# Attention scores in float32r row tiles of 32, with the maxima taken off by a product of their own

## The chip, the cores and the metric

One core of a Trainium2 chip runs the whole kernel. The metric is the device time of one execution in microseconds (us), lower is better. A core has a matrix engine (PE, TensorE), VectorE (DVE), ScalarE (ACT), GpSimd (POOL) and SyncE (SP, which here only issues DMAs). They run side by side and meet at semaphores.

## What is computed

A transformer block over x of shape (4, 512, 128): layer norm, attention with 16 heads of 8 dimensions, a second layer norm and residual, then a gated feed-forward part with layer norm and residual. All is float32. The part that the change touches is the score product and its softmax:

```python
q = (x @ Wq + bq).reshape(b, t, H, hd).transpose(0, 2, 1, 3)
k = ((x @ Wk + bk) @ Wl + bl).reshape(b, t, H, lhd).transpose(0, 2, 1, 3)
v = ((x @ Wv + bv) @ Wl + bl).reshape(b, t, H, lhd).transpose(0, 2, 1, 3)
attn = jax.nn.softmax(jnp.einsum('bhqd,bhkd->bhqk', q, k) * scale, axis=-1)
out = jnp.einsum('bhqk,bhkd->bhqd', attn, v)
```

Here b = 4, H = 16, hd = 8, t = 512. The biases of q and k are large, so the scores need more than bfloat16 accuracy and the row maxima have to be taken off before the exponential.

## The kernel before

Everything is written out by hand: one instruction list per engine, with semaphores between them.

**Groups and blocks.** The 16 heads go in NG = 4 groups of GH = 4. A batch (one of 4) is BLK = 16 blocks: block n belongs to group n // 4 and to key tile t = n % 4 (128 keys). In one block PE does, for each of the 4 heads, one score product for the exponentials (L1262: keys on partitions, 512 queries as columns, into `psB`, which has two banks) and one for the maxima (L1243: queries on partitions, 512 keys as columns, into `psA`, two pairs of banks, of a group that lies LEAD = 6 blocks ahead). Then it multiplies the exponentials of the block before by v (`times_v`, L1274: four heads side by side in column tiles of 32, float32). DVE reduces each pair of `psA` banks to row maxima (L933), two reductions a block. ACT takes each `psB` bank through the exponential (L784), four a block, into `pT`.

**How the scores are made exact enough.** q and k are each split in three bfloat16 parts (`PARTS` = 3). `QS[g]` and `KS[g]` hold in partitions 0 to 71 the nine products of parts by 8 dimensions, zeros up to 95 (KMAX = 96), and in partitions 96 to 98 of `QS` the three bfloat16 parts of the row maxima, against -1 in `KS`. So one bfloat16 product of 96 partitions gives the scores for the maxima, and one of 99 partitions gives the scores less their maxima.

**How the parts get there.** ACT copies q and k out of PSUM twice (L703, L704), POOL (DVE for batch 0) makes the rests (L520, L524, L889 to L898), ACT the second parts (L715); SP writes the parts to DRAM scratch (`q_scr`, `k_scr`, L382) and reads them back, repeated over partitions (L401, L407), 4 DMAs a group. `take_parts` (L696) of batch b waits until batch b-2 has been written (L702).

**Order before the first exponentials.** All four batches' q, k and v are made first, between the first 6 blocks of maxima (the lead, L1310 to L1321). SP's list is: the writes of batch 0, the loads of its four groups, the writes of batch 1 (L440), `put_maxima(0, 0)` (L441), the writes of batches 2 and 3. The first exponential score product waits for `put_maxima(0, 0)`, and that for ACT's `take_first_maxima`, which stands in ACT's list behind `take_q(3)` (L752).

**The maxima of a group.** After its 8 reductions POOL splits them in three parts (`split_maxima`), PE transposes them (`job_m`, L1205), ACT copies (`take_maxima`, L734), SP puts them in place with one DMA (`put_maxima`, L414); the first score product of that group waits for it (L1252).

**Jobs.** Output projection, layer norms and feed-forward of the batch before are placed between the score products, by the table PE_AT (block, place); place 0 is ahead of `for_maxima(1, 0)`, place 1 ahead of `for_exponentials(2)`, place 2 ahead of `for_exponentials(3)`, place 3 ahead of `times_v`, place 4 behind it.

Score bank 0 of `psB` serves heads 0 and 2 and bank 1 heads 1 and 3, so PE's `for_exponentials(2)` waits for the exponential of head 0, and `for_exponentials(3)` for that of head 1 (L1261). In the last 6 blocks of the last batch there are no maxima left, and heads 2 and 3 use `psA`.

Of the kernel before, what the change touches and what calls it, by code (L numbers as in the profile page):

```python
# [23 lines left out]
def sandwich_kernel(nc, x, Wq, bq, Wk, bk, Wv, bv, Wl, bl, Wo, bo, W_r, W_k, W_v, mu_r, mu_k, out):  # L24
    fp32 = mybir.dt.float32
    bf16 = mybir.dt.bfloat16
    u32 = mybir.dt.uint32
# [3 lines left out]
    ds = bass.ds  # L31
# [11 lines left out]
    ROWS = PARTS * PARTS * D  # L43
    KMAX = 96
    KEXP = KMAX + PARTS
# [3 lines left out]
    MINUS_ONES = 0xBF80BF80  # L49

    ctx = ExitStack()
    with ctx:
# [8 lines left out]

        q_scr = nc.dram_tensor("q_scr", [NB, PARTS, D, H, T], bf16, kind="Internal").ap()
        k_scr = nc.dram_tensor("k_scr", [NB, PARTS, D, H, T], bf16, kind="Internal").ap()
# [32 lines left out]
        qf = sb("qf", [P, T])  # L97
        qr = sb("qr", [P, T])
        qp = sb("qp", [P, 2, PARTS, T], bf16)
        kf = sb("kf", [P, T])  # L100
        kr = sb("kr", [P, T])
        kp = sb("kp", [P, 2, PARTS, T], bf16)
# [3 lines left out]
        QS = [sb(f"QS{g}", [P, GH, T], bf16) for g in range(NG)]  # L106
        KS = [sb(f"KS{g}", [P, GH, T], bf16) for g in range(NG)]
# [68 lines left out]
        s_padp = sem("s_padp")  # L176
        s_padv = sem("s_padv")
# [18 lines left out]
        q_r1 = sem("q_r1")  # L196
        q_p1 = sem("q_p1")
        q_p2 = sem("q_p2")
        k_rdy = sem("k_rdy")
        k_tak = sem("k_tak")  # L200
        k_r1 = sem("k_r1")
        k_p1 = sem("k_p1")
        k_p2 = sem("k_p2")
# [3 lines left out]
        q_wr = [sem(f"q_wr{b}") for b in range(NB)]  # L207
        k_wr = [sem(f"k_wr{b}") for b in range(NB)]
        ld = [sem(f"ld{g}") for g in range(NG)]
        LW = PARTS + 1  # L210
# [140 lines left out]

        def later(n):

            return not isinstance(n, int) or n > 0
# [13 lines left out]
        def _(sp):  # L368
# [16 lines left out]
            def write_q(b, i):  # L385
                write_part(b, i, q_scr, qp, (q_tak, q_p1, q_p2)[i], q_wr)

            def write_k(b, i):
                write_part(b, i, k_scr, kp, (k_tak, k_p1, k_p2)[i], k_wr)

            def write_parts(b):
                for i in range(PARTS):
                    write_q(b, i)
                    write_k(b, i)

            def load_q(b, g):
                q_src = q_scr[ds(b, 1), :, :, GH * g:GH * (g + 1), :]
                for i in range(PARTS):
                    r = PARTS * D * i  # L400
                    sp.dma_start(QS[g][r:r + PARTS * D, :, :].rearrange("p h n -> p (h n)"),  # L401
                                 q_src[:, i:i + 1, :, :, :].rearrange("a i d h n -> a (i d) (h n)")
                                 .broadcast_to([PARTS, D, GH * T])).then_inc(ld[g], 16)

            def load_k(b, g):
                k_src = k_scr[ds(b, 1), :, :, GH * g:GH * (g + 1), :]
                sp.dma_start(KS[g][0:ROWS, :, :].rearrange("p h n -> p (h n)"),  # L407
                             k_src.rearrange("a i d h n -> a (i d) (h n)")
                             .broadcast_to([PARTS, PARTS * D, GH * T])).then_inc(ld[g], 16)
# [1056 lines left out]
```

## Time and profile before

| | |
|---|---|
| median of 3 timed runs | 294.33 us (292.95 to 294.61) |
| span of the profiled execution | 292.1 us |
| PE busy | 257.6 us (88%) |
| DVE busy | 218.2 us (75%) |
| ACT busy | 180.4 us (62%) |
| POOL busy | 108.1 us (37%) |
| DMA, mean | 54 GB/s |

The span is from the first to the last instruction of one profiled execution; the page gives no other time for that execution, and the median of the timed runs lies 2.2 us above the span.
### The profile page before, as it was taken

How to read it: one execution, taken by the hardware profiler on the slowest of the kernel's cores; microseconds unless marked ns; L12 is line 12 of the kernel's file. 1: busy time of each engine (PE TensorE's matmuls, PEld its weight loads, DVE VectorE, ACT ScalarE, POOL GpSimd, SP SyncE). 2: the span in 40 equal slices, each digit the busy share in tenths (PEclk: the TensorE clock that was granted, in tenths of full speed). 3: DMA queues.
4: the chain of work that ended last, by engine and by line, in shares of the span. 5: the costliest groups of instructions: out<-in, count | busy, mean ns of one | idle time of the engine just before them, and what ended most of it. 6: DMA issues, size and time to landing. Idle time of an engine off the chain costs nothing.

```text
span 292.1 us, 4845 instructions
## 1 busy us (share of the span) xinstructions
PE 257.6 (88%) x1379; PEld 100.2 (34%) x1379; DVE 218.2 (75%) x384; ACT 180.4 (62%) x351; POOL 108.1 (37%) x236
## 2 busy tenths in 40 slices
PE   7764883099999999999999999999999999898980
PEld 2441541022323232432433334233333433333560
DVE  2695494065888787989889889988998988763545
ACT  2334350566787867687776776777677678695041
POOL 4897370321001011066321344552117155324522
PEclk9686699558999999999999999999999999999798
DMA  4331133160111111110101121010102000000101
GB/s 108 108 109 77 77 125 123 52 198 2 61 39 66 42 46 56 33 77 19 68 27 57 33 88 49 33 66 20 68 12 103 17 1 2 4 1 0 36 2 36
DMA packets 13045, 15.64 MB, mean 54 GB/s; under 512 B 2529, under 2 KB 10722, under 8 KB 13026
## 3 DMA queue, kind: packets, MB, share of 16 engines
q1 hardware_dynamic: 12450, 15.15, 15.5%
q10 hardware_dynamic: 576, 0.26, 0.3%
q8 instruction: 9, 0.15, 0.2%
q14 instruction: 10, 0.08, 0.1%
HBM read 11.01 MB, written 4.19 MB: 52 GB/s over the span
## 4 chain that ended last, share of the span: by engine, by line
PE 72%; DMA 9%; DVE 8%; SPq 4%; ACT 3%; issue 3%; POOL 1%; POOLq 0%; DVEq 0%; ACTq 0%
PE psO L1274 20%; PE psB L1262 20%; PE psA L1243 17%; DMA q_scr<-qp 4%; DVE mx L933 4%; PE psM L1167 3%; PE psM L1173 3%; SPq L382 3%; DMA KS<-k_scr 3%; PE psA L1154 2%; PE psB L1396 1%; DVE er L996 1%; DMA x_all<-in_L_attn_x_dram 1%; PE psO L1186 1%; SPq L401 1%
## 5 line engine op out<-in xcount | busy, mean ns | idle before, releaser
L933 DVE TENSOR_REDUCE mx<-psA 128x2 f32<-128x1024 f32 x128 | 150.8, 1216 | 45.2 <-PE psA L1243 44.8
L784 ACT ACTIVATE pT<-psB 128x512 f32<-128x512 f32 x244 | 133.1, 597 | 41.2 <-PE psB L1262 40.4
L1262 PE MATMUL psB<-QS,KS 99*128 99x512 bf16 x244 | 94.7, 393 | 12.3 <-DMA QS<-mmT 11.9
L1243 PE MATMUL psA<-KS,QS 96*128 96x512 bf16 x256 | 90.7, 391 | 5.7 <-DMA KS<-k_scr 4.4
L1274 PE MATMUL psO<-pT,Vg 128*32 128x512 f32 x512 | 69.1, 611 | 0.4
L1262 PEld LDWEIGHTS psB<-QS,KS 99*128 99x128 bf16 x244 | 23.6, 98 | 92.0 <-ACT pT L784 57.3
L1243 PEld LDWEIGHTS psA<-KS,QS 96*128 96x128 bf16 x256 | 25.2, 100 | 28.7 <-DVE mx L933 6.2
L493 POOL TENSOR_TENSOR mm<-mx,one 128x16 bf16<-128x16 f32 x16 | 3.5, 217 | 43.2 <-DVE mx L933 43.2
L1274 PEld LDWEIGHTS psO<-pT,Vg 128*32 128x32 f32 x512 | 10.2, 108 | 21.8 <-issue 16.9
L532 POOL TENSOR_TENSOR Vg<-v_st,one 128x128 f32<-128x128 f32 x16 | 6.3, 399 | 28.0 <-PE psO L1274 28.0
L703 ACT ACTIVATE qf<-psO,vec 128x512 f32<-128x512 f32 x4 | 2.7, 687 | 18.0 <-DMA q_scr<-qp 13.4
L1154 PE MATMUL psA<-warm 128*128 128x512 bf16 x36 | 11.4, 482 | 1.2 <-DVE warm L905 1.2
L996 DVE RECIPROCAL er<-rr 128x128 f32<-128x128 f32 x12 | 10.7, 924 | 2.3 <-POOL rr L639 2.3
L760 ACT COPY o_sb<-psO 128x512 f32<-128x512 f32 x15 | 8.8, 590 | 4.4 <-PE psO L1274 4.4
L884 DVE TENSOR_SCALAR xh<-x_all,mv_x,rs_x 128x128 f32<-128x128 f32 x16 | 8.0, 653 | 1.9 <-POOL rs_x L500 1.8
L1173 PE MATMUL psM<-ident,o_sb 128*128 128x128 f32 x60 | 9.0, 272 | 0.0
L694 ACT COPY xhT<-psB 128x512 f32<-128x512 f32 x4 | 2.3, 586 | 10.6 <-PE psB L1179 10.6
L520 POOL TENSOR_TENSOR qr<-qf,qp 128x512 f32<-128x512 f32 x3 | 3.5, 1155 | 14.1 <-ACT qp L704 14.1
L1173 PEld LDWEIGHTS psM<-ident,o_sb 128*128 128x128 f32 x60 | 7.5, 141 | 2.9
L506 POOL TENSOR_TENSOR ve_y<-mv_y,eps 128x4 f32<-128x4 f32 x3 | 0.6, 202 | 20.9 <-DVE mv_y L875 20.9
L506 POOL TENSOR_TENSOR ve_f<-mv_f,eps 128x4 f32<-128x4 f32 x3 | 0.6, 201 | 20.5 <-DVE mv_f L875 20.5
L734 ACT COPY mmT<-psM 48x128 bf16<-48x128 bf16 x15 | 3.8, 254 | 4.9 <-PE psM L1205 4.9
(179 smaller groups left out, 293.8 us busy)
## 6 DMA issues: line engine op xcount, KB each, us to landing
QS<-q_scr SPq DMA_DIRECT2D x48, 96.0 KB
KS<-k_scr SPq DMA_DIRECT2D x16, 288.0 KB
q_scr<-qp SPq DMA_DIRECT2D x12, 128.0 KB, 2.3
k_scr<-kp SPq DMA_DIRECT2D x12, 128.0 KB, 2.3
x_all<-in_L_attn_x_dram SPq DMA_DIRECT2D x4, 256.0 KB, 3.4
out_dram<-out_sb SPq DMA_DIRECT2D x3, 256.0 KB, 4.0
QS<-mmT SPq DMA_DIRECT2D x16, 12.0 KB
out_dram<-out_sb SPq DMA_DIRECT2D x2, 128.0 KB, 1.8
```

Source lines behind the costliest of these rows:

```text
L382: sp.dma_start(scr[b, i, :, :, :].rearrange("d h n -> h d n"), parts[:, b % 2, i, :]).then_inc(written[b], 16)
L760: nc.scalar.copy(o_sb[:, :], psO[:, :]).then_inc(o_tak, 1)
L784: nc.scalar.activation(pT[:, n % 2, i, :], score_bank(n, i, last), ACT.Exp, scale=SCALE).then_inc(e_rdy, 1)
L884: last = nc.vector.tensor_scalar(xh[:, b, t, :], x_all[:, b, E * t:E * (t + 1)], mv_x[:, b, t, 0:1], rs_x[:, b, t:t + 1], ALU.subtract, AL ...
L933: nc.vector.tensor_reduce(out=mx[:, g % 2, c:c + 2], in_=psA[:, u, :, :], axis=AX.X, op=ALU.max).then_inc(a_max, 1)
L996: nc.vector.reciprocal(er[:, E * t:E * (t + 1)], rr[:, E * t:E * (t + 1)])\
L1154: nc.tensor.matmul(psA[:, 1, 0, :], warm[:, 0:P], warm[:, :], start=True, stop=True)
L1167: last = nc.tensor.matmul(psM[:, E * t:E * (t + 1)], lhs[:, P * t:P * (t + 1)], rhs, start=True, stop=True)
L1173: last = nc.tensor.transpose(psM[:, P * t:P * (t + 1)], src(t), ident[:, :])
L1243: score = nc.tensor.matmul(psA[:, u, j, :], QS[g][0:KMAX, h, P * t:P * (t + 1)], KS[g][0:KMAX, h, :], start=True, stop=True)
L1262: nc.tensor.matmul(score_bank(n, i, last), KS[g][0:KEXP, i, P * t:P * (t + 1)], QS[g][0:KEXP, i, :], start=True, stop=True).then_inc(b_rdy, 1)
L1274: last = nc.tensor.matmul(psO[QUAD * i:QUAD * (i + 1), :], Vg[:, g, t, i, :], pT[:, n % 2, i, :], start=(t == 0), stop=(t == NT - 1))
```

## The change

q and k are each split in two halves of 12 bits (`HALVES` = 2) by a bit mask: DVE masks the upper half (`top_half`), and POOL (DVE for batch 0) subtracts it for the lower. ACT copies q and k out of PSUM once. The halves stay in SBUF for all batches (`q_hl`, `k_hl`). There is no DRAM scratch: SP copies rows from SBUF to SBUF, eight DMAs a group (four for q, four for k; 32 partitions of 2 KB each), so that the 4 products of halves by 8 dimensions of one head fill 32 partitions, and the four heads of a group the 128. Each score product is one float32r matmul on the 32 partitions of its head.

The maxima are no longer rows of the score product. `MS[g]` holds their three bfloat16 parts at partitions 32i to 32i+2, and a second product of 3 partitions (`less_maxima`), with a tile of -1, adds them into the same bank. They are put there by three DMAs instead of one. The maxima are made in another order (heads 2 and 3, then heads 0 and 1, of one query tile, where it was four query tiles of one head), and `for_maxima(1, 1)` stands ahead of place 1, where it stood behind `for_exponentials(2)`.

```diff
-            def write_part(b, i, scr, parts, made, written):
-                sp.wait_ge(made, 2 * b + 2 if i == 0 else b + 1)
-                sp.dma_start(scr[b, i, :, :, :].rearrange("d h n -> h d n"),
-                             parts[:, b % 2, i, :]).then_inc(written[b], 16)
+            def load_rows(b, g, dst, src, j, half):
+                sp.dma_start(dst[g][j:P:SPREAD, :].bitcast(fp32),
+                             src[QUAD * g:QUAD * (g + 1), half, ds(b * T, T)]).then_inc(ld[g], 16)
+            def load_q(b, g):
+                for j in range(SPREAD):
+                    load_rows(b, g, QS, q_hl, j, j // HALVES)
+            def load_k(b, g):
+                for j in range(SPREAD):
+                    load_rows(b, g, KS, k_hl, j, j % HALVES)
+            def put_maxima(n, g):
+                sp.wait_ge(m_tak, n + 1)
                 for i in range(PARTS):
-                sp.dma_start(QS[g][KMAX:KEXP, :, :].rearrange("p h n -> p (h n)"),
-                             mmT[:, :]).then_inc(m_in, 16)
+                    sp.dma_start(MS[g][i:P:QUAD, :],
+                                 mmT[MC * i:MC * (i + 1), :]).then_inc(m_in, 16)
...
-            write_parts(1)
             put_maxima(0, 0)
-            for b in range(2, NB):
-                write_parts(b)
...
+                for full, parts, hi, lo in ((qf, q_hl, q_hi, q_lo), (kf, k_hl, k_hi, k_lo)):
+                    pool.wait_ge(hi, b + 1)
+                    at = slice(T * b, T * (b + 1))
+                    nc.gpsimd.tensor_tensor(parts[:, 1, at], full[:, b % 2, :], parts[:, 0, at],
+                                            ALU.subtract).then_inc(lo, 1)
...
-                if b >= 1:
-                    act.wait_ge(r1, b)
                 if b >= 2:
-                    act.wait_ge(written[b - 2], 16 * PARTS)
-                nc.scalar.activation(full[:, :], ps[:, :], ACT.Identity, bias=bias).then_inc(taken, 1)
-                nc.scalar.activation(parts[:, b % 2, 0, :], ps[:, :], ACT.Identity,
+                    act.wait_ge(lo, b - 1)
+                nc.scalar.activation(full[:, b % 2, :], ps[:, :], ACT.Identity,
                                      bias=bias).then_inc(taken, 1)
...
+            def top_half(b, full, parts, taken, hi):
+                dve.wait_ge(taken, b + 1)
+                nc.vector.tensor_scalar(parts[:, 0, T * b:T * (b + 1)].bitcast(u32),
+                                        full[:, b % 2, :].bitcast(u32), TOP_BITS, None,
+                                        ALU.bitwise_and).then_inc(hi, 1)
...
+            SPLITS = {0: (top_q, 1), 1: (top_k, 1), 2: (top_q, 2), 3: (top_k, 2), 4: (top_q, 3),
+                      5: (top_k, 3)}
             for a in range(LEAD):
                 for u in range(2):
                     maxima(a // GH, a, a // GH, a % GH, u, False)
+                split, b = SPLITS[a]
+                split(b)
...
-                score = nc.tensor.matmul(psA[:, u, j, :], QS[g][0:KMAX, h, P * t:P * (t + 1)],
-                                         KS[g][0:KMAX, h, :], start=True, stop=True)
+                rows = rows_of(PAIRS[u] + j)
+                score = nc.tensor.matmul(psA[:, u, j, :], QS[g][rows, P * t:P * (t + 1)],
+                                         KS[g][rows, :], start=True, stop=True)
...
-                nc.tensor.matmul(score_bank(n, i, last), KS[g][0:KEXP, i, P * t:P * (t + 1)],
-                                 QS[g][0:KEXP, i, :], start=True, stop=True).then_inc(b_rdy, 1)
+                nc.tensor.matmul(score_bank(n, i, last), KS[g][rows_of(i), P * t:P * (t + 1)],
+                                 QS[g][rows_of(i), :], start=True, stop=False)
+
+            def less_maxima(n, i, last):
+                rows = slice(QUAD * i, QUAD * i + PARTS)
+                nc.tensor.matmul(score_bank(n, i, last), neg[rows, :], MS[n // NT][rows, :],
+                                 start=False, stop=True).then_inc(b_rdy, 1)
...
                     for_exponentials(0)
                     for_maxima(0, 0)
+                    less_maxima(n, 0, last)
                     for_exponentials(1)
                     for_maxima(0, 1)
+                    less_maxima(n, 1, last)
                     jobs(n, 0)
                     for_maxima(1, 0)
+                    for_maxima(1, 1)
                     jobs(n, 1)
                     for_exponentials(2)
-                    for_maxima(1, 1)
+                    less_maxima(n, 2, last)
                     jobs(n, 2)
                     for_exponentials(3)
+                    less_maxima(n, 3, last)
```

The tiles that only the old form needed go too: the padding of `QS` and `KS` with zeros and -1 (POOL L541, DVE L902), ACT's second copies (L704, L715).

## Rows read from the trace of the kernel before

**Rows 1.** The page: busy share of the engines, granted clock in 40 slices.
```profile
PE 257.6 (88%) x1379; PEld 100.2 (34%) x1379; DVE 218.2 (75%) x384; ACT 180.4 (62%) x351; POOL 108.1 (37%) x236
PE   7764883099999999999999999999999999898980
PEclk9686699558999999999999999999999999999798
```

**Rows 2.** Lines by form: shapes, count | busy us, mean ns | idle before, releaser.
```profile
L933 DVE TENSOR_REDUCE mx<-psA 128x2 f32<-128x1024 f32 x128 | 150.8, 1216 | 45.2 <-PE psA L1243 44.8 <-issue 0.2
L784 ACT ACTIVATE pT<-psB 128x512 f32<-128x512 f32 x244 | 133.1, 597 | 41.2 <-PE psB L1262 40.4
L1262 PE MATMUL psB<-QS,KS 99*128 99x512 bf16 x244 | 94.7, 393 | 12.3 <-DMA QS<-mmT 11.9 <-ACT pT L784 0.2
L1243 PE MATMUL psA<-KS,QS 96*128 96x512 bf16 x256 | 90.7, 391 | 5.7 <-DMA KS<-k_scr 4.4 <-DVE mx L933 1.1
...
L520 POOL TENSOR_TENSOR kr<-kf,kp 128x512 f32<-128x512 f32 x3 | 3.5, 1155 | 1.0 <-ACT kp L704 0.9
```

**Rows 3.** Timeline of one block without jobs: start us, us, engine, line, operation.
```profile
82.31 0.39 PE L1262 MATMUL psB<-QS,KS 99*128 99x512 bf16 x1
...
82.54 0.38 PE L1243 MATMUL psA<-KS,QS 96*128 96x512 bf16 x1
82.54 0.10 PEld L1262 LDWEIGHTS psB<-QS,KS 99*128 99x128 bf16 x1
82.74 2.17 ACT L784 ACTIVATE pT<-psB 128x512 f32<-128x512 f32 x4 [0.58 <-PE psB L1262]
...
83.41 0.38 PE L1262 MATMUL psB<-QS,KS 99*128 99x512 bf16 x1
...
83.88 0.39 PE L1262 MATMUL psB<-QS,KS 99*128 99x512 bf16 x1
...
84.20 1.06 PE L1274 MATMUL psO<-pT,Vg 128*32 128x512 f32 x8
...
85.19 0.39 PE L1262 MATMUL psB<-QS,KS 99*128 99x512 bf16 x1
```

**Rows 4.** Timeline of PE: a job, first score products of batches 1, 2, a float32 job.
```profile
106.98 0.60 PE L1173 MATMUL psM<-ident,o_sb 128*128 128x128 f32 x4
...
109.38 0.39 PE L1262 MATMUL psB<-QS,KS 99*128 99x512 bf16 x1
...
163.50 0.39 PE L1262 MATMUL psB<-QS,KS 99*128 99x512 bf16 x1
...
255.08 1.11 PE L1225 MATMUL psM<-xk,w_T 128*128 128x512 f32 x2
```

**Rows 5.** The chain that ended last, before the first exponentials: start us, us, what.
```profile
22.10 7.90 DMA KS<-k_scr
...
43.89 10.30 DMA q_scr<-qp
...
55.73 2.27 DMA QS<-mmT
```

**Rows 6.** Timeline of the start: kf copied, rest, x normalised, DMA issues, first product.
```profile
14.74 0.69 ACT L703 ACTIVATE kf<-psM,b_kl 128x512 f32<-128x512 f32 x1 [1.29 <-PE psM L1192]
...
16.07 0.68 DVE L892 TENSOR_TENSOR kr<-kf,kp 128x512 f32<-128x512 f32 x1
...
16.63 1.24 SPq L382 DMA_DIRECT2D q_scr<-qp  x2
...
23.33 3.27 DVE L884 TENSOR_SCALAR xh<-x_all,mv_x,rs_x 128x128 f32<-128x128 f32 x8 [0.29 <-POOL rs_x L500]
...
58.12 0.58 PE L1262 MATMUL psB<-QS,KS 99*128 99x512 bf16 x1 [11.91 <-DMA QS<-mmT]
```

**Rows 7.** One stretch by engine: us, busy (count) of each, granted clock, DMA share.
```profile
60.00:70.00 10.00, 10.00 (x36) 2.42 (x34) 6.36 (x6) 5.92 (x11) 1.19 (x5) 0.60 0.39 114
```

**Rows 8.** The tile `mmT`: issues of its DMA, ns minimum/median/maximum.
```profile
L414 SPq DMA_DIRECT2D QS<-mmT x16: 698/747/797, 55.7 to 252.6; - x16
```

More of the change, by code:

```diff
@@ L26, in sandwich_kernel @@
     bf16 = mybir.dt.bfloat16
+    f32r = mybir.dt.float32r
     u32 = mybir.dt.uint32
@@ L42, in sandwich_kernel @@
     PARTS = 3
[L43 to L45 removed]
+    HALVES = 2
+    SPREAD = HALVES * HALVES
     QUAD = 32
@@ L96, in sandwich_kernel @@
         xhT = sb("xhT", [P, 2, T])
[L97 to L102, printed above, removed]
+        qf = sb("qf", [P, 2, T])
+        kf = sb("kf", [P, 2, T])
+        q_hl = sb("q_hl", [P, HALVES, NB * T])
+        k_hl = sb("k_hl", [P, HALVES, NB * T])
         v_st = sb("v_st", [P, NB, NT * H * D])
-        QS = [sb(f"QS{g}", [P, GH, T], bf16) for g in range(NG)]
-        KS = [sb(f"KS{g}", [P, GH, T], bf16) for g in range(NG)]
+        QS = [sb(f"QS{g}", [P, T], f32r) for g in range(NG)]
+        KS = [sb(f"KS{g}", [P, T], f32r) for g in range(NG)]
+        MS = [sb(f"MS{g}", [P, T], bf16) for g in range(NG)]
+        neg = sb("neg", [P, P], bf16)
         Vg = sb("Vg", [P, NG, NT, GH, QUAD])
@@ L423, in _ @@
                 load_x(b)
-            write_q(0, 0)
-            write_k(0, 0)
-            write_q(0, 1)
-            write_q(0, 2)
-            write_k(0, 1)
-            write_k(0, 2)
-            sp.wait_ge(q_wr[0], 16 * PARTS)
-            for g in range(NG):
-                sp.wait_ge(s_padp, (1, 4, 7, 10)[g])
-                if g == 0:
-                    sp.wait_ge(s_padv, 2)
+            for dst, src, hi, lo in ((QS, q_hl, q_hi, q_lo), (KS, k_hl, k_hi, k_lo)):
+                for half, made in enumerate((hi, lo)):
+                    sp.wait_ge(made, 1)
+                    for j in range(SPREAD):
+                        if (j // HALVES if dst is QS else j % HALVES) == half:
+                            load_rows(0, 0, dst, src, j, half)
+            for g in range(1, NG):
                 load_q(0, g)
-                if g == 0:
-                    sp.wait_ge(k_wr[0], 16 * PARTS)
                 load_k(0, g)
-            write_parts(1)
             put_maxima(0, 0)
-            for b in range(2, NB):
-                write_parts(b)
-            for b in range(1, NB):
-                sp.wait_ge(q_wr[b], 16 * PARTS)
-                sp.wait_ge(k_wr[b], 16 * PARTS)
+            sp.wait_ge(q_lo, NB)
+            sp.wait_ge(k_lo, NB)
+            sp.wait_ge(q_hi, NB)
+            sp.wait_ge(k_hi, NB)
             def batch(b, first, last):
@@ L925, in _, with maxima @@
             x_normalise(3)
-            def maxima(group, a, g, h, u, free):
+            def maxima(group, a, g, t, u, free):
                 dve.wait_ge(a_rdy, a * 2 + (u + 1))
-                if h == 0 and u == 0 and free:
+                if t == 0 and u == 0 and free:
                     dve.wait_ge(m_p2, group - 1)
-                c = NT * h + 2 * u
-                nc.vector.tensor_reduce(out=mx[:, g % 2, c:c + 2], in_=psA[:, u, :, :],
+                h = PAIRS[u]
+                into = mx[:, g % 2, :].rearrange("p (h t) -> p h t", t=NT)[:, h:h + 2, t]
+                nc.vector.tensor_reduce(out=into, in_=psA[:, u, :, :],
                                         axis=AX.X, op=ALU.max).then_inc(a_max, 1)
@@ L1234, in job_f, with rows_of, scores_for_maxima @@
                 product_by_tile(kact, w_T[:, T_WVF, :], f_rdy)
-            def scores_for_maxima(e, a, g, h, u, j, free=False):
-                if u == 0 and j == 0 and h == 0:
+            def rows_of(h):
+                return slice(QUAD * h, QUAD * (h + 1))
+            def scores_for_maxima(e, a, g, t, u, j, free=False):
+                if u == 0 and j == 0 and t == 0:
                     pe.wait_ge(ld[g], (e + 1) * (16 * LW))
```

132 lines of the change are left out of this document (38 added, 94 removed).

## The prediction

> **What bounds the kernel now.** I read the page first, for the engine shares and the granted clock. PE is busy in nearly every slice from 60 us on, DVE 75% and ACT 62% over the whole, and the clock sinks only in the first quarter [rows 1]. So there are two parts to price: the start, up to the first score product for exponentials at 58.12 us [rows 6], and the steady part of 64 blocks behind it.
>
> In the steady part I went from the forms [rows 2] to one block without jobs [rows 3]. It runs from 82.31 to 85.19: 2.88 us. Two sums give the same 2.88. By PE alone: products start 0.22 apart (82.31 to 83.41 is five of them), eight take 1.76, the last one keeps `times_v` waiting 0.32 instead of 0.22, and `times_v` takes 0.99 (84.20 to 85.19). That is 1.76 + 0.03 of waiting + 0.10 + 0.99. By the exponentials: the first score product starts at 82.31, ACT begins at 82.74 (0.43 later), two exponentials take half of the 2.17, 1.09, the product of head 3 starts 0.05 behind the second of them (83.88), then 0.32 and 0.99. That is 0.43 + 1.09 + 0.05 + 0.32 + 0.99 = 2.88. Work taken from PE alone thus gives nothing: this second chain stays. DVE needs 2.4 us a block for two reductions (2 x 1.216 [rows 2]) and is not the bound in such a block. A middle batch takes 163.50 - 109.38 = 54.1 us [rows 4]; 16 x 2.88 = 46.1, so its jobs cost 8.0.
>
> At the start two stretches of waiting stand out in the chain: the load of `KS` (7.90 us) and a write of `q_scr` (10.30 us), which holds ACT, and behind it the first maxima [rows 5]. The first product waited 11.91 us [rows 6].
>
> **The change part by part: a steady block.** It adds four products (`less_maxima`), twelve in place of eight. Each must follow its own score product, in the same rows and the same bank, so it can't lie beside it: 0.22 each. Two of them are on the chain of the exponentials whatever else overlaps: that of head 0 ahead of the first exponential, that of head 3 ahead of `times_v`. The chain becomes 0.22 + 0.43 + 1.09 + 0.05 + 0.22 + 0.32 + 0.99 = 3.32 us, 0.44 more.
>
> Whether PE itself fits in that depends on the row tiles. The trace of before has no row tile and no float32r. The nearest row for tiles is `times_v`: eight instructions of 512 columns, four column tiles of two float32 instructions each, in 0.99 us [rows 3]. One float32 product of 512 columns on the full array, two instructions, has 1.11 us [rows 4], so four one after another would need near 4. Tiles do lie side by side here. If row tiles do the same, the twelve products take six slots of 0.22 (first score with first maxima product, then `less_maxima` with the next pair, and so on): 1.3 us, which hides in the 3.32. If they don't, PE is the bound: 12 x 0.22 + 0.10 + 0.99 = 3.73. The price of a block is thus between 3.32 and 3.73; below 3.32 it can't go unless `less_maxima` costs nothing. I take 3.32, since the nearest row shows tiles side by side. For a float32r product the bound from below is the bfloat16 spacing of 0.22, from above the float32 product, 1.0; one of its two instructions, about 0.45, lies between. I take 0.22: it is a single instruction of four-byte numbers whose mantissas are cut to 12 bits, which stands nearer to the bfloat16 row than to the pair that full float32 needs.
>
> On tiles the Trainium skill (TensorE: Matmul & The Clock Gate, Part 3) says that matmuls in different row groups run side by side, and gives 3.07x for four of K = 32 and N = 512; by this the block is at 3.32, and the trace shows the same for column tiles only. The same section says that a weight load overlaps a running matmul only if its row group differs. By that each `less_maxima` would also show its weight load, 0.10 by the row of a load here, and the block would be 3.52. The trace speaks against it: at 82.54 the load for a product of 99 rows runs beside a product of 96 of the same rows [rows 3], and the starts stay 0.22 apart.
>
> **Jobs.** The new block leaves PE idle from 0.86 (its first eight products issued, if side by side) to about 1.24, when the first exponential has freed its bank. Jobs at places 0, 1 and 2 (four transposes take 0.44: 106.98 to the next product [rows 4]) fill this gap in part. But a job uses the full array, so each needs two changes of tiling, which I put at 0.12 each by the 0.10 and 0.12 around `times_v`. Place by place: the four small ones at places 0 to 2 cost 0.2 each or less instead of 0.44, `f` 0.4 instead of 0.9, those at places 3 and 4 their own time plus 0.12. The sum is 5.5 us a batch instead of 8.0.
>
> **Maxima put in place by three DMAs.** One issue takes SP 0.75 us [rows 8], so the last starts 1.5 us later, and it lands 2.3 us after its start [rows 5]. ACT's copy of `m2` and `m4` ends about when block 7 or 15 begins, and the group is needed one block later: 1.5 + 2.3 = 3.8 against 3.32, a wait of 0.5 each. `m1` in batch 0 is 0.5 later still; in later batches the jobs of block 3 hide it. Some 4 us over the kernel. SP is not late elsewhere: 8 loads of a group at 0.6 to 0.75 are 5.5 us and stand ahead of a `put_maxima` that comes three blocks later.
>
> **Steady sum.** Batch 0: 16 x 0.44 = 7.0, waits 1.9, its few jobs -0.5: +8.4. Batches 1 and 2: 16 x 3.32 = 53.1, jobs 5.5, waits 0.9 = 59.5 against 54.1: +5.4 each. Batch 3: ten such blocks +3.4, and six without maxima, where five slots replace four, +1.3. Together +24.
>
> **The start.** Until the copy of kf at 14.74 nothing changes. Then: no second copy by ACT; DVE masks and subtracts (0.45, put between a copy and a subtraction, and 0.68 [rows 6]), done by 16.8. SP issues the first eight copies at 0.62 to 0.75 from 14.7 on, to about 19.9, landed 2 us later. The first scores can start near 22 instead of 30.0. DVE isn't free then: it still has the normalising of x, which ended at 26.6 [rows 6] and moves up by the third parts and casts that it loses and the memsets of POOL beside it, to 24.3. Eight reductions are 9.7, four masks 1.8: the first group's maxima stand at 35.8, the k half of batch 2 is masked last. POOL has its subtraction (1.155 [rows 2]) ahead of the split of the maxima in its list; split 1.2, transpose, copy 0.7, issues 1.5, landing 2.3: the first exponential score product near 43.8 instead of 58.1. The writes of `q_scr` and their 10.3 us are gone. That is -14.3. What is late next: the reductions of DVE, then SP, whose 32 loads end between 35 and 39. The granted clock was 0.60 from 60 to 70 us, mostly the lower of its two levels (1.2 of 1.2 and 2.4 GHz), after PE had stood for 11.9 us [rows 6, 7]; after a wait of 2 us it may not fall. Batch 0 took 109.38 - 58.12 = 51.3 where full clock would give some 49.5: -1.7. The start gives -16; I hold -10 to -20 for possible.
>
> **Sum.** 292.1 + 24 - 16 = 300, with the 2.2 us between span and median 302.3; I say 302.5. Its own range is 295 to 312.
>
> **Rivals.**
> 1. *Row tiles don't overlap here.* A block takes 3.73, and the jobs keep their 8.0 and gain 2.6 of tiling changes: batch 0 +14.5, batches 1 and 2 +16 each, batch 3 +15, the start -16: +46, 340 us. For it: no row shows row tiles, and scores and `less_maxima` mix two types. Against it: `times_v`. 25%.
> 2. *float32r takes as long as one instruction of the float32 pair, 0.43.* With overlap, the chain gets 0.22 more for head 0 and for head 3: 3.76 a block, about 335. Without, PE has 8 x 0.43 + 4 x 0.22 + 1.09 = 5.4 a block, over 430. 12% and 3%.
> 3. *The start pays for all.* The place is the stretch before 58.12: the writes and loads through DRAM vanish. It decides if the first exponential score product comes before 34, or if it comes at 41 and the steady cost is only 16. The chain of reductions alone (24.3 + 9.7) makes the first impossible without DVE freed earlier; the second needs jobs hidden better than I have it. It gives 288 to 291. 8%, and 5% for no difference.
> 4. *The clock falls in the steady part*, since quarter tiles use less of the array: every slot 0.43. Over 400 us. 2%.
>
> **How the numbers follow.** Forecast (side by side, 0.22, slower) 45%; the rivals 25, 15, 8 + 5 and 2%. The range of 8 in 10 leaves out the worst cases (5%) and most of rival 3: 293 to 342. A measurement of this kernel can tell about 0.5% from no change. Faster by over 0.5%: 8%; within: 5%; slower: 87%.
>
> **What would show it.** Side by side: starts of a score product and of the maxima product behind it well under 0.22 apart; else rival 1. The distance from a score product of head 0 to its exponential: 0.65, where it is 0.43. Block period 3.3 (forecast), 3.7 (rival 1 or 2). First exponential score product at 44. Waits for the DMA of `mmT` of 0.5 about twice a batch. DVE less busy by share than 75%. The prediction is wrong if the product of head 3 no longer waits for the exponential of head 1, or if the period of a block is under 3.2.

## The result, and the profile after

The changed kernel takes 423.13 us (median of 4 executions, 422.91 to 425.22) where the kernel before takes 294.47 (4 executions, 292.95 to 295.38): a ratio of 1.4375, 95% interval 1.4313 to 1.4437. The profiled execution has a span of 421.1 us against 292.1, so 129.0 us are to be found. The forecast was 302.5 with a range up to 342. The sign was right and the size was not: the time is that of rival 4, which had 2%.

From the page of the changed kernel: busy share of the engines, and PE's share and the granted clock in 40 slices. It answers to [rows 1].

```profile
span 421.1 us, 5372 instructions
PE 392.9 (93%) x1633; PEld 148.6 (35%) x1635; DVE 217.5 (52%) x386; ACT 175.2 (42%) x337; POOL 92.4 (22%) x221
PE   7888999999999999999999999999999999999893
PEclk9895555555555555556655555556655565557989
```

DVE and ACT do the same number of microseconds of work as before (217.5 and 175.2, before 218.2 and 180.4). PE's went from 257.6 to 392.9, and the last line says why: the granted clock stands near 0.5, the lower of its two levels (1.2 and 2.4 GHz), in nearly all of the span from the fourth slice to the 36th. Before it was at full level in nearly all slices from the tenth on [rows 1]. The mean over the span is 0.592, before 0.932.

The costliest groups of the same page (busy us, mean ns of one, idle before and its releaser), which answer to [rows 2]:

```profile
L869 DVE TENSOR_REDUCE mx<-psA 128x2 f32<-128x1024 f32 x128 | 152.1, 1220 | 162.6 <-PE psA L1186 162.4
L716 ACT ACTIVATE pT<-psB 128x512 f32<-128x512 f32 x244 | 133.0, 596 | 167.8 <-PE psB L1213 162.3
L1207 PE MATMUL psB<-QS,KS 32*128 32x512 f32 x244 | 115.4, 757 | 12.0 <-ACT pT L716 12.0
...
L1213 PE MATMUL psB<-MS,neg 3*128 3x512 bf16 x244 | 97.0, 616 | 0.0
```

One reduction and one exponential are as long as before (1220 and 596 ns; 1216 and 597 in [rows 2]), but both engines now wait about 162 us for PE, before about 45 and 40. In these lines `f32` is also what the float32r products show, one instruction each (numbers of four bytes, here halves of 12 bits); L1207 and L1186 are the score and the maxima products, L1213 is `less_maxima`, L1225 `times_v`.

Two stretches side by side, in the columns of [rows 7] (us, busy and count of PE, PEld, DVE, ACT, POOL, granted clock, DMA share, GB/s). First a middle batch of the kernel before, then the same batch of the changed one:

```profile
121.31:175.24 53.93, 53.69 (x311) 19.51 (x311) 48.43 (x77) 39.28 (x77) 21.23 (x52) 1.00 0.14 51
```
```profile
147.77:242.75 94.98, 91.35 (x375) 32.92 (x374) 49.49 (x76) 40.15 (x77) 21.22 (x52) 0.54 0.10 26
```

By such marks (the first score product for exponentials, then in three batches the start of the job that multiplies `w_in` by `oT`) the 129.0 us lie as follows: start 58.12 to 39.42, -18.7; first product to first mark 63.2 to 108.35, +45.2; two batches 107.7 to 189.7, +82.0; the rest 63.1 to 83.6, +20.5.

A block without jobs, timeline of the changed kernel (start us, us, engine, line, operation), which answers to [rows 3]:

```profile
54.46 0.79 PE L1207 MATMUL psB<-QS,KS 32*128 32x512 f32 x1
54.46 0.79 PE L1186 MATMUL psA<-KS,QS 32*128 32x512 f32 x1
54.47 0.79 PE L1207 MATMUL psB<-QS,KS 32*128 32x512 f32 x1
54.47 0.79 PE L1186 MATMUL psA<-KS,QS 32*128 32x512 f32 x1
55.06 0.65 PE L1213 MATMUL psB<-MS,neg 3*128 3x512 bf16 x2
...
55.74 1.09 ACT L716 ACTIVATE pT<-psB 128x512 f32<-128x512 f32 x2 [0.92 <-PE psB L1213]
...
58.05 1.94 PE L1225 MATMUL psO<-pT,Vg 128*32 128x512 f32 x8
59.91 0.79 PE L1207 MATMUL psB<-QS,KS 32*128 32x512 f32 x1
```

Four products in four row tiles start within 0.01 us of each other, so row tiles do lie side by side; rival 1 is out. But the block takes 59.91 - 54.46 = 5.45 us in place of 2.88, `times_v` 1.86 in place of 0.99, and the first exponential starts 1.28 after its score product in place of 0.43.

Where does the clock fall? In the lead, and from there to about 380 us it comes back only for moments of a few us, of which one is shown (columns as above):

```profile
30.00:32.00 2.00, 0.62 (x4) 0.33 (x4) 2.00 (x4) 0.58 (x2) 2.00 (x3) 1.00 0.40 108
32.00:34.00 2.00, 2.00 (x6) 0.74 (x6) 2.00 (x3) 0.52 (x1) 0.80 (x2) 0.87 0.39 105
34.00:36.00 2.00, 1.26 (x7) 0.17 (x5) 0.33 (x1) 0.16 (x1) 1.37 (x5) 0.50 0.38 100
...
192.00:194.00 2.00, 2.00 (x13) 1.12 (x6) 0.00 (x0) 0.72 (x2) 0.00 (x0) 0.53 0.04 10
194.00:196.00 2.00, 1.47 (x14) 0.79 (x12) 0.75 (x1) 1.31 (x3) 0.78 (x1) 1.00 0.00 0
196.00:198.00 2.00, 2.00 (x6) 0.82 (x6) 2.00 (x3) 1.47 (x3) 0.26 (x1) 0.83 0.00 0
198.00:200.00 2.00, 2.00 (x10) 0.20 (x8) 2.00 (x3) 0.60 (x1) 0.30 (x1) 0.50 0.34 87
```

At 30 us DVE is the bound (2.00 of 2.00) and PE stands most of the time; after that the clock is low, as it was before after PE had stood 11.9 us [rows 6, 7]. The difference is that before it rose again in ordinary blocks, by 70 us, and here it does not. At 191.02 `times_v` begins and at 192.88 a job, both with weights and data that are float32 over all 128 rows; the clock is high after it and low again by 198, behind the score products of one block (194.44 to 197.09).

The start itself went as argued, only further. The chain that ended last, before the first exponential score product (start us, us, what), in answer to [rows 5]:

```profile
27.90 2.27 DVE mx L869 x2
30.17 0.43 DVE q_hl L824
30.60 2.27 DVE mx L869 x2
32.87 0.34 DVE k_hl L824
...
33.28 1.26 POOL k_hl L485
...
39.47 0.74 PE psB L1207
```

### The profile page after: what moved, and what is told of

Read it like the earlier page. It is cut to its first block, busy times and chain, and to the rows that moved or that the text cites. A ratio compares the mean times of both kernels' runs of the same rounds, so it can differ in the third digit from the quotient of the medians.

```text
span 421.1 us, 5372 instructions
## 1 busy us (share of the span) xinstructions
PE 392.9 (93%) x1633; PEld 148.6 (35%) x1635; DVE 217.5 (52%) x386; ACT 175.2 (42%) x337; POOL 92.4 (22%) x221
## 4 chain that ended last, share of the span: by engine, by line
PE 83%; ACT 6%; DVE 6%; issue 2%; POOL 1%; DMA 1%; POOLq 0%; DVEq 0%
PE psO L1225 27%; PE psB L1207 24%; PE psB L1213 13%; ACT pT L716 6%; PE psM L1113 5%; PE psM L1107 4%; PE psA L1186 3%; DVE mx L869 2%; PE psM L1165 1%; PE psA L1094 1%; DVE xh L816 1%; PE psB L1351 1%; DMA x_all<-in_L_attn_x_dram 1%; PE psM L1145 1%; POOL rs_x L466 1%
## 5 line engine op out<-in xcount | busy, mean ns | idle before, releaser
L869 DVE TENSOR_REDUCE mx<-psA 128x2 f32<-128x1024 f32 x128 | 152.1, 1220 | 162.6 <-PE psA L1186 162.4
L1207 PE MATMUL psB<-QS,KS 32*128 32x512 f32 x244 | 115.4, 757 | 12.0 <-ACT pT L716 12.0
L1225 PE MATMUL psO<-pT,Vg 128*32 128x512 f32 x512 | 117.3, 1007 | 0.2 <-ACT pT L716 0.2
L1186 PE MATMUL psA<-KS,QS 32*128 32x512 f32 x256 | 99.5, 817 | 1.9 <-DVE mx L869 1.9
L1213 PE MATMUL psB<-MS,neg 3*128 3x512 bf16 x244 | 97.0, 616 | 0.0
L1207 PEld LDWEIGHTS psB<-QS,KS 32*128 32x128 f32 x244 | 46.3, 271 | 133.5 <-ACT pT L716 74.8
L1186 PEld LDWEIGHTS psA<-KS,QS 32*128 32x128 f32 x256 | 38.6, 291 | 8.8 <-issue 5.0
L1213 PEld LDWEIGHTS psB<-MS,neg 3*128 3x128 bf16 x244 | 23.5, 135 | 35.8 <-issue 33.7
L1225 PEld LDWEIGHTS psO<-pT,Vg 128*32 128x32 f32 x512 | 12.6, 137 | 27.1 <-issue 22.3
L1113 PE MATMUL psM<-ident,o_sb 128*128 128x128 f32 x60 | 16.3, 425 | 0.0
L581 POOL TENSOR_TENSOR dx<-xs 128x512 f32<-128x512 f32 x3 | 3.1, 1034 | 31.8 <-ACT xs L700 31.8
L586 POOL TENSOR_TENSOR rr<-er,one 128x512 f32<-128x512 f32 x3 | 3.1, 1038 | 23.7 <-ACT er L708 23.7
```

The source lines that it names most:

```text
L869: nc.vector.tensor_reduce(out=into, in_=psA[:, u, :, :], axis=AX.X, op=ALU.max).then_inc(a_max, 1)
L1113: last = nc.tensor.transpose(psM[:, P * t:P * (t + 1)], src(t), ident[:, :])
L1186: score = nc.tensor.matmul(psA[:, u, j, :], QS[g][rows, P * t:P * (t + 1)], KS[g][rows, :], start=True, stop=True)
L1207: nc.tensor.matmul(score_bank(n, i, last), KS[g][rows_of(i), P * t:P * (t + 1)], QS[g][rows_of(i), :], start=True, stop=False)
L1213: nc.tensor.matmul(score_bank(n, i, last), neg[rows, :], MS[n // NT][rows, :], start=False, stop=True).then_inc(b_rdy, 1)
L1225: last = nc.tensor.matmul(psO[QUAD * i:QUAD * (i + 1), :], Vg[:, g, t, i, :], pT[:, n % 2, i, :], start=(t == 0), stop=(t == NT - 1))
```

## The experiments

All times are of one execution each unless more are named; the kernel before took 294.4 to 294.7 (median) beside them. Most forecasts below gave one time for a clock that is low throughout and one for a clock that is high throughout; the measured clocks were often mixed, and then the time lay between the two.

**Which product costs the time: the changed kernel without `less_maxima`.** It leaves out that the maxima are taken off.

```
-  QS[g][rows_of(i), :], start=True, stop=False)
+  QS[g][rows_of(i), :], start=True, stop=True).then_inc(b_rdy, 1)
-  less_maxima(n, 0, last)          (and the other three calls)
```

> The changed kernel without the less_maxima products (the maxima aren't taken off). Theory A with the 3-partition products as the culprit: clock back at 1.0 and about 285 us. Theory A with the 32-partition tiles as the culprit, and theory G: clock stays at 0.5; a block loses the two products on its chain, each 0.4 to 0.6 us at half clock, so 4.4 to 4.7 us a block and 350 to 375 us.

291.62 us, mean clock 0.892. The clock is low from 44 to 83 us and then high to the end:

```profile
PEclk9599795555579999999999999999999999999596
```

A middle batch takes 55.1 us. With the 32-row float32r products alone the clock was low for 40 us and then high for the rest of the kernel. The time lies between the two that were forecast, about 285 and 350 to 375, and near the first. The edit takes away the products of 3 rows, but also four products in every block; the experiments on rows below separate the two.

**Rows without the new products: the kernel before, its scores over 32 rows.** It leaves out two thirds of the rows of the sum. The second kernel takes other 32 rows for each head, those of one of the four row tiles, so its sums are other parts again.

```
-  KS[g][0:KEXP, i, P * t:P * (t + 1)],  QS[g][0:KEXP, i, :]
+  KS[g][0:QUAD, i, P * t:P * (t + 1)],  QS[g][0:QUAD, i, :]      (maxima product likewise)
   second: QUAD*i:QUAD*(i+1), and QUAD*((t+2)%4):QUAD*((t+2)%4+1) for the maxima
```

> The kernel before, with every score product cut to partitions 0 to 31 (bfloat16, all in the same row tile, one after another; the other parts and the maxima are left out of the sums). Starts stay 0.22 us apart at full clock, so PE is as busy in time as before. Theory A (the granted clock follows how much of the array the products use): the clock falls to 0.5 in the steady part as in the changed kernel, a block takes about 5.5 us, the whole 420 to 450 us. Theory G (it follows the share of time in which PE streams columns, so waits and tiling changes count): clock 1.0 and 294 us, within 3. Theory T (it is the float32r type): 294 us too.

> The kernel before with bfloat16 score products of 32 partitions, spread over the four row tiles (the sums are parts of the scores only). Compared with the same products in one tile it lets them run side by side, which leaves PE more idle. Theory A: clock 0.5, 370 to 430 us. Theory G: clock 0.5 here although the products in one tile kept 1.0. Theory T: clock 1.0 and 285 to 294 us.

349.45 us, mean clock 0.772, and 303.88 us, 0.838. The same instructions, types and order as before, with 32 rows in place of 96 and 99 and all in one tile, cost 55 us. The clock line of the first, and two stretches of it by engine:

```profile
PEclk9886556555555555555599999999999999989987
```
```profile
164.00:168.00 4.00, 4.00 (x12) 1.42 (x10) 1.23 (x1) 2.26 (x5) 0.00 (x0) 0.50 0.01 3
...
172.00:176.00 4.00, 4.00 (x24) 1.13 (x21) 2.96 (x9) 2.79 (x6) 2.97 (x8) 0.99 0.15 46
```

At 164 to 168 PE is busy 4.00 of 4.00 and the clock is 0.50. It is low from 56 us on, with PE busy in all of it from 60 on, and rises at 172, behind the first jobs of batch 1 (float32 over the full array, the longest from 168.52 to 170.5); then it stays high. With 96 and 99 rows it rose at 68 us in ordinary blocks, though PE had stood longer ahead of them (11.9 us, here 2.5). So a busy PE alone doesn't bring the level back. The spread version is low until about 122 us, where such a job ran (121.60), and then high; in both the clock stays high with 32-row products once it is there. Both times are misses: the first lies between the 294 and the 420 to 450 that the theories gave, since the low level lasted for a third of the kernel, and the second between its 294 and 370. Each is a single execution.

**Only the rows of `less_maxima`, 3 or 32.** Both kernels set `neg` and `MS` to zero outside three rows of each tile; one multiplies all 32 rows (the added 29 are zeros, the sum is the same), the control multiplies three.

```
+  link_n(nc.gpsimd.memset(neg[:, :], 0.0))                     (both)
+  link_n(nc.gpsimd.memset(neg[QUAD*i:QUAD*i + PARTS, :], -1.0))
+  link_n(nc.gpsimd.memset(MS[g][:, :], 0.0))
-  rows = slice(QUAD * i, QUAD * i + PARTS)
+  rows = rows_of(i)                                            (not in the control)
```

> The changed kernel with less_maxima over all 32 partitions of its row tile (29 of them zero on both sides), where it has 3; instructions, order and sums are the same. Theory A1 (the clock follows the rows of the array that products really use): the clock is back at 1.0 for most of the steady part, as without less_maxima, and the time 300 to 325 us. Theory A2 (what counts is how long products run and in which tiles, not how many rows carry numbers): clock 0.5 and 415 to 425 us as in the changed kernel.

> The changed kernel with less_maxima over all 32 partitions of its tile again, now timed, since the look before gave 337 us with stretches at either clock. If the level that the clock takes is decided by the work of the kernel, the runs agree to 1% (334 to 340 us). If it hangs on chance near the point where the level changes, they spread over 310 to 400 us.

> The control for that one: the same extra memsets of MS and of the tile of -1 at the start, but less_maxima over 3 partitions as in the changed kernel. If the rows of less_maxima made the difference: clock 0.5 in the steady part, 418 to 428 us. If it was the other start (a later or earlier first product): 330 to 345 us.

With 32 rows: 337.04 us at a mean clock of 0.849, and in four more executions 326.25, 355.03, 345.86 and 310.49, at 0.886, 0.775, 0.813 and 0.947. The control: 427.06 and 414.56 (0.585, 0.613), as the changed kernel (four executions, 0.587 to 0.593). This is the one comparison with several executions on both sides, and they don't overlap: with 3 rows six executions of 414.6 to 427.1 us, with 32 rows five of 310.5 to 355.0. Zeros in 29 more rows of one of three kinds of products are worth about 85 us. The times with 32 rows go with the clock and spread by 45 us; only the shortest lies in the forecast 300 to 325. What decides in an execution how long the level stays low was not found. From the first execution, the clock line of the page, and a middle batch at full clock:

```profile
PEclk9999855579755555985879999999999999999898
```
```profile
205.75:268.18 62.43, 57.34 (x376) 23.82 (x375) 48.77 (x76) 39.92 (x77) 21.28 (x52) 1.00 0.15 39
```

This batch tells what the change costs apart from the clock: 62.4 against 53.9 before, +8.5. A block at full clock, the same kernel's timeline:

```profile
192.13 0.49 PE L1219 MATMUL psB<-QS,KS 32*128 32x512 f32 x1
192.14 0.50 PE L1198 MATMUL psA<-KS,QS 32*128 32x512 f32 x1
192.47 0.39 PE L1225 MATMUL psB<-MS,neg 32*128 32x512 bf16 x2
192.97 1.09 ACT L728 ACTIVATE pT<-psB 128x512 f32<-128x512 f32 x2 [1.12 <-PE psB L1225]
...
194.11 0.50 PE L1219 MATMUL psB<-QS,KS 32*128 32x512 f32 x1
194.46 0.39 PE L1225 MATMUL psB<-MS,neg 32*128 32x512 bf16 x1
194.78 1.06 PE L1237 MATMUL psO<-pT,Vg 128*32 128x512 f32 x8
195.77 0.50 PE L1219 MATMUL psB<-QS,KS 32*128 32x512 f32 x1
```

195.77 - 192.13 = 3.64 us, where the forecast had 3.32.

**More rows by full products.** In one kernel `less_maxima` is a single product over 128 rows (zeros outside the head's three); in the other both score products read all 128 rows, which adds the other heads to each score.

```
   less_maxima:  -  neg[rows, :]            +  neg[0:P, i, :], MS[n // NT][0:P, :]
   scores:       -  KS[g][rows_of(i), ...]  +  KS[g][0:P, ...]   (and QS)
```

> The changed kernel with less_maxima as one product over all 128 partitions of MS, with -1 only at the three rows of its head; same result. It can't run beside a row tile and costs tiling changes of about 0.1 us each. Theories A1 and A2: clock 1.0; a block is six slots of products more than the changed one, 4.0 to 4.4 us, 330 to 355 us. If the clock stays at 0.5 none of them holds.

> The changed kernel with every float32r score product over all 128 partitions (the sum of four heads, so the scores are others), one after another; less_maxima stays at 3 partitions. More work in time and in the array. Theories A and G: clock 1.0 in the steady part, a block of 12 products at 0.22 plus 1.09 is 3.7 us or a little more, 325 to 345 us, much faster than the 423 us of the changed kernel. Theory T: clock 0.5 as in the changed kernel and over 450 us.

362.40 us at a mean clock of 0.945, and 398.21 at 0.976. The second has the full level from 40 us on, the first from about 65 us on (it is at 0.52 from 40 to 64). Both are still far slower than before, and slower than forecast (330 to 355 and 325 to 345). A full product doesn't lie beside a tile of 32 rows: in the first kernel it starts 0.43 behind the pair. With full scores a block is 4.91 us at clock 1.00 (123.94 to 128.85). Timeline of PE, score and maxima products of that block:

```profile
123.94 0.50 PE L1207 MATMUL psB<-QS,KS 128*128 128x512 f32 x1
124.28 0.39 PE L1186 MATMUL psA<-KS,QS 128*128 128x512 f32 x1
...
125.90 0.73 PE L1186 MATMUL psA<-KS,QS 128*128 128x512 f32 x2
126.47 0.40 PE L1207 MATMUL psB<-QS,KS 128*128 128x512 f32 x1
```

Two prices stand in it. A product behind a change of tiling starts 0.32 behind the one ahead of it, in place of 0.22: about 0.1 for each change, and this block has eight. And a float32r product that is the first behind products of another kind keeps the next float32r product waiting 0.34 (123.94 to 124.28, 125.90 to 126.24), the second only 0.23 (126.24 to 126.47); over the whole trace it is 0.34 in 157 of such first pairs and 0.23 in 49 of the later ones. This block has four of these first products, 0.11 each. Together 12 x 0.22 + 8 x 0.1 + 4 x 0.11 + 0.99 = 4.87. The forecast had neither the second price nor as many changes.

**Fillers: thrown-away full products ahead of the scores of each block.** Two in one kernel, five in the other.

```
+  if i == 0:
+      for _ in range(2):     # 5 in the other
+          nc.tensor.matmul(score_bank(n, i, last), warm[:, 0:P], warm[:, :],
+                           start=True, stop=True)
```

> The changed kernel with two extra bfloat16 products of 128 partitions and 512 columns ahead of the first score product of each block (thrown away). More work, 0.43 us a block at full clock and one more tiling change. Theories A1 and A2: clock 1.0 in most of the steady part, a block 3.9 to 4.2 us, 325 to 350 us, so faster than the changed kernel although it does more. If the clock doesn't follow the work in the array: clock 0.5, a block 0.86 to 1 us longer than 5.5, 475 to 490 us.

> The changed kernel with five thrown-away products of 128 partitions ahead of each block, where two gave 438 us and a mean clock of 0.68. If it is the share of the array at work that decides: clock 1.0 in nearly the whole steady part, a block 3.6 + 5 x 0.22 + 0.1 = 4.8 us, 375 to 395 us, faster than with two. If the products that are added do not count: clock 0.6 to 0.7, over 500 us.

438.38 us at a mean clock of 0.678, and 407.54 at 0.897. The first was a miss: two fillers raise the clock only at times and cost their own work and two changes of tiling (325 to 350 was forecast). Five raise it nearly everywhere (a block of 4.82 us at 1.00), so the kernel with three more products in each block took less time, though more than the 375 to 395 forecast, since the mean clock stayed at 0.84 to 0.92 from 40 to 300 us. With one execution of each, and the spread just seen, the 31 us between them are not proof; the clock line of the second is:

```profile
PEclk9798978989789998889898889678989999899987
```

**The type: the changed kernel's products as bfloat16.** The score products read the upper half of each 32-bit word, in the same tiles and order; the lower part of the mantissas is left out.

```
+  def top(tile):
+      return tile[:, :].bitcast(bf16).rearrange("p (n two) -> p n two", two=2)[:, :, 1]
-  KS[g][rows_of(i), ...]
+  top(KS[g])[rows_of(i), ...]      (QS, and the maxima product, likewise)
```

> The changed kernel with the score products reading only the upper 16 bits of each number, as bfloat16, in the same places, tiles and order (the lower bits are left out). If float32r is what keeps the clock low: clock 1.0, near 300 us. If it is the small share of the array: clock 0.5 to 0.6 as in the changed kernel, 405 to 420 us, and only the distance from a score product to its less_maxima tells the types apart: 0.34 us at full clock (0.59 at half) in the changed kernel, 0.22 to 0.26 (0.43) here.

363.81 us at a mean clock of 0.687; it came between what the two theories gave. The clock is low through all of batch 0 and comes and goes after it; a stretch of batch 0 by engine, and one block at the low level, timeline:

```profile
60.00:120.00 60.00, 57.99 (x250) 10.59 (x249) 28.43 (x30) 27.28 (x52) 3.76 (x15) 0.50 0.09 24
```
```profile
203.18 0.60 PE L1210 MATMUL psB<-QS,KS 32*128 32x512 bf16 x1
203.59 0.64 PE L1216 MATMUL psB<-MS,neg 3*128 3x512 bf16 x2
...
208.22 0.60 PE L1210 MATMUL psB<-QS,KS 32*128 32x512 bf16 x1
```

So bfloat16 products in these tiles leave the clock low too: float32r isn't needed for it. It adds its part: at the low level `less_maxima` of a head starts 0.41 behind its score product (203.18 to 203.59), with float32r 0.60 (54.46 to 55.06 above), and a block is 5.04 in place of 5.45. That the kernel also spent more time at the high level may come from this, or be the spread; it wasn't separated.

**The start alone, in the kernel before.** If the 18.7 us came from moving the first maxima ahead, the kernel before should be able to take some of it. The parts get four buffers in place of two, so that ACT doesn't wait for the writes of batch 0, and SP puts the first maxima in place earlier.

```
-  qp = sb("qp", [P, 2, PARTS, T], bf16)      +  qp = sb("qp", [P, NB, PARTS, T], bf16)   (kp too)
-  act.wait_ge(written[b - 2], 16 * PARTS)
   SP:  -  write_parts(1)                     +  put_maxima(0, 0)
        -  put_maxima(0, 0)                   +  write_parts(1)
   second: put_maxima(0, 0) ahead of the loads of groups 2 and 3 of batch 0
   third:  as the second, the writes of batches 2 and 3 behind the loads of groups 1 and 2
```

> The kernel before with two things about its start only: the parts of q and k have a buffer for each batch (four in place of two), so ACT doesn't wait for the writes of batch 0, and SP puts the first maxima in place ahead of the writes of batch 1. Nothing in the steady part changes. The first score product for exponentials should start at 45 to 48 us in place of 58.1, and the time be 281 to 285 us. If the start is held by something else (the loads of the later groups, or the writes that now come later), 290 to 294 us.

> The kernel before with four buffers, and SP's put_maxima(0, 0) ahead of the loads of groups 2 and 3 (in the run before it stood behind them, and its DMA took 8.1 us to land in place of 2.3). If the loads in the same queues held it: the first score product for exponentials at 48 to 49 us in place of 54.0, 282 to 285 us. If groups 2 and 3 are late for their maxima then: no gain over 289.

> The kernel before with four buffers, the first maxima ahead of the loads of groups 2 and 3, and the writes of batches 2 and 3 between the later maxima and loads, so that no put_maxima stands behind twelve of them (in the run before, the second one came at 69.1 us and PE waited 8.8). First exponential score product at 46.4, second group without a long wait, clock high from there: 280 to 284 us. If the loads of group 2 are late for their maxima (3.1 us of waiting in the run before) and the rest holds: 284 to 287.

The medians, with the ratio of fast executions on record, which is not the quotient of the medians: 289.22 against 294.41 (ratio 0.9795, 0.9725 to 0.9865); 295.24 against 294.50 (1.003, 0.9994 to 1.0067); 289.56 against 294.72 (0.9843, 0.9742 to 0.9945). The first starts its exponentials at 53.99 and not at 45 to 48, since the copy of the maxima, which stands behind the loads of all four groups in SP's list, now lands late; from its chain:

```profile
45.45 0.26 ACT mmT L731
...
45.72 8.14 DMA QS<-mmT
...
53.99 0.59 PE psB L1259
```

The copy took 8.14 us where it took 2.27 before [rows 5]. The second removes that, begins at 46.42 at full clock, and gives it all back: the next loads and the next maxima stand behind it in SP's list.

```profile
46.42 0.38 PE L1260 MATMUL psB<-QS,KS 99*128 99x512 bf16 x1 [0.56 <-DMA QS<-mmT]
...
55.31 0.39 PE L1241 MATMUL psA<-KS,QS 96*128 96x512 bf16 x1 [3.05 <-DMA KS<-k_scr]
...
71.33 0.61 PE L1260 MATMUL psB<-QS,KS 99*128 99x512 bf16 x1 [8.79 <-DMA QS<-mmT]
```

The third takes the writes out of the way and is bound by the loads of group 2 (8.24 us of DMA in its chain at 47.75). None of the three reached its forecast of 281 to 285, 282 to 285 and 280 to 287. The first and the third, about 2% below the kernel before, are the fastest versions found and can't be told apart by these intervals; they take part of the gain of the start and leave the products at 96 and 99 rows.

## Why the prediction was wrong

**The failed step is the clock of the steady part.** The steady sum was made at the durations of a kernel that runs at full level, and rival 4 was given 2% with half a sentence. Rows that spoke for it were on the table: the clock of before sinks when PE stands and takes until about 70 us to return [rows 1, 7], so its level depends on what PE does, and by the listing each of the new products uses a quarter of the array or 3 rows of it. What the runs showed in its place: after the lead the level is low, and whether it returns goes with how many rows of the array are at work, and a busy PE isn't enough. The kernel before with 32 of its rows (clock 0.772 for 0.935) and the 3 and 32 rows of `less_maxima` (0.585 to 0.613 and 0.775 to 0.947) change the rows and little else, and the clock follows; the full products point the same way (0.945 and 0.976), but change the order in time too. Without `less_maxima` the clock returns at 84 us (0.892). That it is worse than four tiles side by side because it works with 3 rows where the next pair could run is my reading; that its rows count is measured. How the hardware measures this was not settled by the runs; only its direction was.

Sizes: of the two middle batches' +82.0, 2 x 8.5 = 17 are there at full clock (the 62.43 us batch above), 65 are the clock's. Taking each of the four batches at +8.5, an estimate, the steady part would cost +34, and 129.0 = -18.7 + 34 + 113.7: the clock costs about 114. The 8.5 are measured with 32 rows in `less_maxima`; in the moment at high level after 194 us the changed kernel itself has 0.34 between a score product and its `less_maxima` (194.44 to 194.78), the other one 0.35 (194.11 to 194.46). By the same estimate, the clock taken as before, the changed kernel at full level would take 294.5 - 18.7 + 34 = 310, near the 310.49 of the shortest execution with 32 rows.

**Point by point.**
- *Row tiles lie side by side*: right, 0.01 us between the starts. The Trainium skill (TensorE: Matmul & The Clock Gate, Part 3), which says that different row groups run together, holds here. Its rule that a weight load overlaps a matmul only of a different row group isn't borne out by the bfloat16 kernel: there `less_maxima` starts 0.41 behind its score product of the same rows at the low level, and at this level bfloat16 products of the kernel before that follow each other start 0.43 apart (60.21 to 60.64), so no load shows.
- *A float32r product takes 0.22*: 0.34 to its own `less_maxima`, and also to a following float32r product where it is the first of its kind; 0.23 only from the second on. This term was mis-sized. The chain of a block has it twice, at heads 0 and 3: the first exponential starts 0.84 behind the product where 0.65 was forecast (+0.19), and `less_maxima` of head 3 starts 0.35 behind its product where 0.22 was forecast (+0.13). That is the 0.32 by which 3.64 is above 3.32. Whether the longer weight load of float32r (0.18 us at 192.13, where the bfloat16 load of `less_maxima` has 0.09) makes it was not tried.
- *Two of the four `less_maxima` are on the chain of the exponentials*: right; ACT waits for L1213.
- *Jobs 5.5 a batch*: 62.4 - 16 x 3.64 = 4.2. They hide better in the longer block. A middle batch at full clock is +8.5 where +5.4 was forecast; of these 3.1 the blocks give 16 x 0.32 = +5.1, the jobs -1.3, the waits of the next point -0.9, together +2.9.
- *Waits of 0.5 for the DMA of `mmT`*: PE has none in the changed kernel, where a block of 5.45 us covers the 3.8 from copy to landing, and with 32 rows in `less_maxima` only one, of 1.17, ahead of the first exponential score product.
- *The start, -14.3*: -18.7. The first maxima product came at 20.98 (forecast 22), the normalising of x ended at 22.7 (24.3), its eight reductions at 32.87 (30.60 + 2.27) and the mask behind them at 33.21 (forecast 35.8), the product came at 39.42 (43.8). So 2.6 of the 4.4 come from DVE, and 1.8 from what follows. PE did not stand waiting for the landing there: ahead of the product its chain has its own list, 2.00 us of L1139 from 36.74 and a pair of maxima products from 38.74. Up to 33.21 DVE is what binds, as said; a mask takes 0.42 (forecast 0.45).
- *After a wait of 2 us the clock may not fall*: that wait did not decide. The clock was low by 34 us, before the first exponential score product, behind 30 to 32 us, in which PE was busy 0.62 of 2.00.

The period of a block, 5.45, fits rival 4 and also rival 2 without overlap (5.4); the four starts 0.01 apart and the granted clock tell them apart. The list of signs should have begun with the row of the granted clock.

## What to carry to other kernels

When products are cut into smaller tiles, price them at both levels of the clock: count the rows at work, those of the smallest product above all, and look at the granted clock behind stretches in which PE has stood: does the work that follows bring it back? Then a few zero rows can be worth a fifth of the time, as in this kernel, and one execution isn't enough to tell. A gain at the start holds only when what stood behind it in the queues moves up as well: in the second kernel with an early start one copy moved ahead gave 12 us, and they were lost to the next.

## What the runs showed of the hardware

- With bfloat16 score products of 32 rows the granted clock stayed at 0.50 from 60 to 172 us, with PE busy in all of it; with 96 and 99 rows it came back at 68 (one profiled execution each).
- Rows that hold only zeros count: 29 of them in the product that takes off the maxima made 421 us (the median of two executions, 414.56 and 427.06) into 310 to 355 (five).
- The same kernel can differ by 45 us between executions (310.49 to 355.03), with the mean clock between 0.947 and 0.775.
- A change between the full array and a tile costs about 0.1 us: 0.32 between starts in place of 0.22 (full scores, `less_maxima` to the next score product).
- Four products in four row tiles start within 0.02 us of each other, float32r (54.46 to 54.47) and bfloat16 (203.18 to 203.20).
- A float32r product of 512 columns over 128 rows keeps the next one waiting 0.34 us when it is the first behind products of another kind (157 pairs), and 0.23, nearly as bfloat16, from the second on (49 pairs).
